# The reciprocal root of the variance moves from ScalarE to GpSimd

## The chip, the cores and the metric

The kernel runs on one core of a Trainium2 chip. The metric is the device time of one execution in microseconds (us). The kernel before takes 2158.09 us (median of three runs, 2158.0 to 2159.71). Five engines work side by side, each through its own queue of instructions in order: PE (TensorE, matrix multiplications; its weight loads are shown as PEld), DVE (VectorE), ACT (ScalarE), POOL (GpSimd) and SP (SyncE, which issues the DMAs here). They meet only at semaphores.

## The reference, cut to what matters

Four "triangle" layers follow each other on an image x of 256 x 256 tokens with 64 channels. Each adds its result to x, after a group normalisation over pairs of channels (`_gn`). Three of the four (layers 0, 1 and 3) begin with a layer norm over the 64 channels of each token:

```python
xn = (x - mean(x)) * rsqrt(var(x) + 1e-5) * g + b         # per token, over 64 channels
left  = xn @ Wl.T * m * sigmoid(xn @ Wlg.T)               # m: a mask per token, layers 0 and 1
right = xn @ Wr.T * m * sigmoid(xn @ Wrg.T)
out_gate = sigmoid(xn @ Wog.T)
out = einsum('bikd,bjkd->bijd', left, right)              # the triangle product
x = x + (layernorm(out) * out_gate) @ Wout.T
```

The change touches only how `rsqrt(var + eps)` of that first layer norm is computed. Layer 2 has no such norm on its input.

## The kernel before, in words

x lies as 128 partitions (two halves of the image, 64 channels each) by 32768 tokens. Each layer has three stages: the projection (`project`, L435; layer 2 has its own), the triangle product, and the output. In the trace the projections of layers 0, 1 and 3 run roughly from 58 to 370 us, 660 to 980 us and 1523 to 1844 us.

`project` takes the tokens in 64 chunks of 512 columns. Sixteen chunks make one turn of a loop (BODY), and eight chunks make one batch (BATCH), so a projection has 8 batches and the program has 24. Each engine has a function `step(i, q, more)` that it runs for every chunk q, with leads: the constants on L444 say how many chunks ahead of the chunk in hand a part is done. The parts are:

- PE, in this order in each step (L602): `spread` of chunk q+4 (NORM), `center` of chunk q+14, `heads` of chunk q for its two rows of 256 tokens, `out_gate` of chunk q, and `variance` of chunk q+13. `variance` (L561) adds the squares over channels into one PSUM tile, VAR; after eight chunks it holds a 16 x 512 tile, one batch. `spread` (L572) multiplies the reciprocal roots out over the channels into PSUM tile R; it first waits for `r_split` of its batch.
- ACT (L661): `square` (two activations, L635 and L637, for chunk q+14), two sigmoids of the gates (L654), `root` where a batch has just been completed (q is 2 or 10), and then the sigmoid of the output gate (L671). `out_gate` of the next chunk on PE waits until that last sigmoid has read the PSUM tile GATE.
- `root` (L639): loads the table set that has logarithm and exponential, waits for the batch's last `variance`, and computes exp(-0.5 * ln(var + eps)) in two activations, L644 and L647. The sigmoid after it needs its own table set again, and a load is placed in front of it.
- DVE (L745): `norm` of chunk q+4 (three or so tensor operations, which wait for `spread`), `split_r` where q+5 is a multiple of 8 (q is 3 or 11), and `left_and_right` of chunk q (L742, two instructions, which wait for the sigmoids and free the PSUM pair that `heads` of the next chunk writes). `split_r` (L691) waits for `r_done` and splits r into three bfloat16 terms by five instructions (L699 to L706).
- POOL, in layers 0 and 1 alone (L761): multiplies the product by the mask, after `left_and_right` of the same chunk. In layer 3 POOL has nothing to do in the projection.

Before the loop, PE and ACT run 14 chunks of `center`, `square` and `variance` alone, and the first `root` and `split_r` of a projection lie there.

Of the kernel before, what the change touches and what calls it, by code (L numbers as in the profile page):

```python
# [28 lines left out]
ALU = mybir.AluOpType  # L29
ACT = mybir.ActivationFunctionType  # L30
AXIS = mybir.AxisListType

P = 128
# [3 lines left out]
CH = 512  # L37
NCH = HALF * S // CH
ROWS = CH // S
SEG = 16  # L40
SCH = SEG // ROWS
BODY = 2 * SCH
BATCH = 8
# [4 lines left out]
LN_SET = "natural_log_exp_and_others"  # L48
# [19 lines left out]
def build(nc, a, out):  # L68

    with ExitStack() as ctx:  # L70
        def sb(name, shape, dt=F32):
            return ctx.enter_context(nc.sbuf_tensor(name, shape, dt))

        def counter(name, base=FIRST):
            return Counter(ctx.enter_context(nc.semaphore(name)), base)

        k = {
            "basis": sb("basis", [P, P]), "var_w": sb("var_w", [P, 4 * BATCH - 2]), "ident": sb("ident", [P, P]),
            "pool_w": sb("pool_w", [P, P]), "last_row": sb("last_row", [2, P]), "unit": sb("unit", [P, 3]),
            "gn": sb("gn", [P, 12]), "gn_stats": sb("gn_stats", [P, NCH, 6]), "gn_sums": sb("gn_sums", [P, 2, NCH]),  # L80
            "vec": sb("vec", [P, NVEC]), "center": sb("center", [P, P]), "shift": sb("shift", [P, 1]),
            "w_out": sb("w_out", [P, P]),
            "out_bias": sb("out_bias", [P, 1]), "one": sb("one", [1, P]),

            "mask": sb("mask", [P, 2, 2, P]),
        }
        ps = [ctx.enter_context(nc.psum_tensor(f"ps{n}", [P, 2, 512], F32)) for n in range(4)]

        c = {n: counter(n) for n in (
            "fold_vec", "fold_mm", "fold_act", "stat_done", "z_done", "sq_done", "var_done", "log_done", "r_done", "r_part", "r_split", "spread_done",  # L90
            "xn_done", "hi_done", "lo_done", "proj_done", "gate_mm_done", "sig_done", "gate_done", "masked", "lr_done", "pair_read",
            "tr_done", "tr_copied", "tri_done", "packed", "o_copied", "o_stored", "o_moved",
            "ln_stat", "ln_root", "ln_scale", "centered", "scaled", "wt_done", "wt_copied", "gated",
            "out_mm_done", "u_cleared", "out_gated", "x_new", "counted", "aggregated")}

        for n, ring in (("const_in", 1), ("x_in", 8), ("lr_out", 2), ("first_out", 2), ("gate_out", 4), ("lr_in", 2),
                        ("xc_in", 4), ("gc_in", 4), ("x_out", 4)):
            for i in range(ring):
                c[f"{n}{i}"] = counter(f"{n}{i}", 16)
        start_counters(nc, c, k, a)  # L100
        first_statistics(nc, a, c, k)
        x = a["x"]
        for n, kind in enumerate(("masked", "masked_bf16", "plain", "normed")):
            x_new = out if n == 3 else a[f"x_dram{n % 2}"]
            layer(nc, n, kind, a, x, x_new, c, k, ps)
            x = x_new
# [95 lines left out]
class Fold:  # L202
# [53 lines left out]
    def step(self, dve, ins):  # L256

        self.steps += 1
        ins.then_inc(self.done.sem, 1)
        dve.wait_ge(self.done.sem, self.done(self.steps))  # L260
# [155 lines left out]
SEG_PARTS = 8  # L416
# [18 lines left out]
def project(nc, n, kind, low, HG, x, a, left_right, blocks, c, k, ps):  # L435
# [5 lines left out]

    LOAD, CENTER, VARIANCE, SPLIT, NORM = 16, 14, 13, 5, 4  # L444
    masked, gate = kind != "normed", a["gate"]
    with ExitStack() as ctx:
        def sb(name, shape, dt=F32):
# [7 lines left out]
        sig, gates = sb("sig", [P, 4, CH]), sb("gates", [P, 4, CH])  # L455
        paired = low == BF16
# [24 lines left out]
        def staged(b, q, row):  # L481

            at = q % SCH * ROWS + row
            return stage[b].rearrange("p g b l n (h i) -> p (g b) (l n h) i", h=HG)[:, :, :, at]
# [145 lines left out]
        def _(act):  # L630
# [8 lines left out]
            def root(i, b):  # L639

                batch = i * (BODY // BATCH) + b
                act.preload_act_table_set(LN_SET)
                act.wait_ge(c["var_done"].sem, c["var_done"](batch * BATCH + BATCH))
                act.activation(log_var[:], VAR, ACT.Ln, bias=k["unit"][0:2 * BATCH, 2:3]).then_inc(c["log_done"].sem, 1)  # L644
                act.wait_ge(c["log_done"].sem, c["log_done"](batch + 1))
                act.wait_ge(c["r_split"].sem, c["r_split"](batch))
                act.activation(r[:], log_var[:], ACT.Exp, scale=-0.5).then_inc(c["r_done"].sem, 1)  # L647

            def gate_pair(i, q, row):
                m = i * BODY + q  # L650
# [107 lines left out]
                norm(0, q)  # L758
            bodies_of(dve, step)

        if masked:  # L761
            @block.gpsimd
            def _(pool):
                def mask_pair(i, q, row):
                    m = i * BODY + q
                    b = q // SCH
                    if q % SCH == 0 and row == 0:

                        pool.wait_ge(c[f"lr_out{b}"].sem, c[f"lr_out{b}"](i * 16 * SEG_PARTS))
                        pool.wait_ge(c[f"first_out{b}"].sem, c[f"first_out{b}"](i * 64))  # L770
                    pool.wait_ge(c["pair_read"].sem, c["pair_read"](m * 2 + row + 1))
                    product = sig[:, (2 * q + row) % 4, :].rearrange("p (a e) -> p a e", a=4)

                    by_g = k["mask"][:].rearrange("p g b i -> p (g b) i")
                    mk = by_g[:, :, bass.ds(m * ROWS + row, 1)].to_broadcast([P, 4, P])
                    pool.tensor_tensor(staged(b, q, row), product, mk,
                                       ALU.mult).then_inc(c["lr_done"].sem, 1)

                def mask_rows(i, q):
                    m = i * BODY + q  # L780
                    b = q // SCH
                    if q % SCH == 0:
                        pool.wait_ge(c[f"lr_out{b}"].sem, c[f"lr_out{b}"](i * 16 * SEG_PARTS))
                        pool.wait_ge(c[f"first_out{b}"].sem, c[f"first_out{b}"](i * 64))
                    pool.wait_ge(c["pair_read"].sem, c["pair_read"](m * 2 + 2))
                    slot, at = 2 * q % 4, q % SCH * ROWS
                    product = sig[:, slot:slot + 2, :].rearrange("p r (c e) -> p c e r", c=4)
                    by_g = k["mask"][:].rearrange("p g b i -> p (g b) i")
                    mk = by_g[:, :, bass.ds(m * ROWS, ROWS)].unsqueeze(2).to_broadcast([P, 4, P, ROWS])
                    rows = stage[b].rearrange("p g b l n (h i) -> p (g b) (l n h) i", h=HG)[:, :, :, at:at + ROWS]  # L790
                    pool.tensor_tensor(rows, product, mk, ALU.mult).then_inc(c["lr_done"].sem, 2)

                with pool.Fori(0, bodies) as i:
                    for q in range(BODY):
                        if paired:
                            mask_rows(i, q)
                        else:
                            for row in range(ROWS):
                                mask_pair(i, q, row)

    fold.finish()
    for s in range(4):
# [621 lines left out]
def constants():  # L1424

    basis = np.zeros((C, C), np.float32)
    for m in range(C - 1):
        basis[:m + 1, m] = 1 / np.sqrt((m + 1) * (m + 2))
        basis[m + 1, m] = -(m + 1) / np.sqrt((m + 1) * (m + 2))
    live = (np.arange(P) % C != C - 1)  # L1430
    group = np.arange(P) % C // 2
    var_w = np.zeros((P, 4 * BATCH - 2), np.float32)
    spread = np.zeros((P, BATCH, P), np.float32)
    for g in range(2):
        half = slice(g * C, g * C + C)
        var_w[half, 2 * BATCH - 2 + g] = live[half] / C
        for q in range(BATCH):
            for part in range(3):
                spread[R_PART * part + 2 * q + g, q, half] = live[half]
    spread[R_ONE] = ~live  # L1440
    unit = np.zeros((P, 3), np.float32)
    unit[:, 0] = ~live
    unit[:, 1] = np.where(live, EPS, 1)
    unit[:, 2] = EPS
    h_center = {}
    for n, H in ((2, 16), (3, C)):
        h_center[f"h_center{n}"] = np.zeros((P, P), np.float32)
        h_center[f"h_center{n}"][:2 * H, :2 * H] = np.kron(np.eye(2), np.eye(H) - 1 / H)
    last_row = np.zeros((2, P), np.float32)
    last_row[0, C - 1] = last_row[1, P - 1] = 1  # L1450
    return {
        **h_center, "basis": np.kron(np.eye(2), basis), "var_w": var_w, "spread": spread.reshape(P, BATCH * P), "ident": np.eye(P),
        "pool_w": (group[:, None] == group[None, :]) / 4, "last_row": last_row, "unit": unit, "one": np.ones((1, P)),
    }
# [90 lines left out]
```

## Time and profile before

| | |
|---|---|
| median of 3 runs | 2158.09 us |
| the profiled execution: its own time | 2161.47 us |
| its span, first to last instruction | 2159.6 us |
| mean granted TensorE clock over the span | 0.96 of full speed |
| busy share of the span: PE, DVE, ACT, POOL | 83%, 71%, 61%, 37% |

A row of the timeline gives the start in us, the duration in us, the engine, the line of the kernel, the operation, what it writes and reads, and how many instructions the row merges. What stands in brackets is the idle time of the engine just before it, and what ended it. A row of the groups ends with busy us in total and the mean in ns, and then the idle time before them.

### The profile page before, as it was taken

Reading aid. Unit: us, or ns where it says so; the run is one execution under the profiler, and the core shown is the slowest. Engines: PE = TensorE matmul, PEld = TensorE weight load, DVE = VectorE, ACT = ScalarE, POOL = GpSimd, SP = SyncE. Lnnn points to the kernel's source line nnn. Section 1 sums busy time; section 2 is a strip of 40 time slices with the busy share of each in tenths; the row PEclk is TensorE's granted clock in tenths of the full one; section 3 lists DMA queues with packets and bytes.
Section 4 is the critical chain, followed back from the end, with each engine's and each line's share of the span. In section 5 each row is a group of like instructions: output and inputs, shape, how many; then the busy total and the mean of one; then the engine's idle time right before and its main releaser. Section 6 shows DMA issues by size and latency. Waiting matters only on the chain. (4 is left out here: it accounts for less than half of the span.)

```text
span 2159.6 us, 40771 instructions
## 1 busy us (share of the span) xinstructions
PE 1792.7 (83%) x10305; PEld 966.5 (45%) x10389; DVE 1522.9 (71%) x3171; ACT 1310.5 (61%) x2413; POOL 808.0 (37%) x740
## 2 busy tenths in 40 slices
PE   0899996897998999965699799877799997699665
PEld 0234343785552343433355476633233333588332
DVE  7588887225754999996876487588488889344775
ACT  0577775466994777755599576433377776344322
POOL 0044445006980444445799100288000000000799
PEclk9999999898999999998899899999899999899999
DMA  7367777775994446446499686299447776754799
GB/s 316 118 190 224 241 217 219 292 311 175 362 369 137 137 156 194 156 147 234 152 366 360 228 293 225 95 396 398 151 149 222 236 231 207 266 232 161 246 354 333
DMA packets 336162, 512.88 MB, mean 237 GB/s; under 512 B 23979, under 2 KB 189486, under 8 KB 329654
## 3 DMA queue, kind: packets, MB, share of 16 engines
q1 hardware_dynamic: 336054, 511.65, 69.3%
q8 instruction: 42, 0.69, 0.1%
q14 instruction: 66, 0.54, 0.1%
HBM read 293.46 MB, written 205.52 MB: 231 GB/s over the span
## 5 line engine op out<-in xcount | busy, mean ns | idle before, releaser
L1289 POOL TENSOR_TENSOR shared<-O,out_rs 128x128 f32<-128x128 f32 (+1 forms) x128 | 94.9, 743 | 687.3 <-DVE out_rs L1196 686.1
L591 PE MATMUL ps<-w_heads,hi 64*128 64x256 f16 x3072 | 292.1, 273 | 36.3 <-DVE sig L742 25.2
L654 ACT ACTIVATE sig<-ps,largest 128x512 f32<-128x512 f32 x384 | 246.8, 692 | 51.3 <-PE ps L591 49.8
L1087 ACT ACTIVATE O<-ps 128x512 f32 (+1 forms) x144 | 151.9, 1055 | 183.5 <-PE ps L1008 183.5
L635 ACT ACTIVATE zs<-ps,shift 128x512 f32<-128x512 f32 x192 | 131.9, 687 | 213.0 <-PE ps L559 213.0
L1333 PE MATMUL ps<-ident,shared 128*128 128x128 f32 (+1 forms) x1024 | 163.3, 284 | 107.9 <-POOL shared L1289 107.8
L1333 PEld LDWEIGHTS ps<-ident,shared 128*128 128x128 f32 (+1 forms) x1024 | 114.3, 133 | 278.3 <-POOL shared L1289 194.2
L591 PEld LDWEIGHTS ps<-w_heads,hi 64*128 64x128 f16 x3072 | 154.1, 95 | 181.3 <-issue 65.8
L559 PE MATMUL ps<-xs,center 128*128 128x512 f32 x384 | 204.7, 615 | 13.6 <-issue 10.4
L591 PE MATMUL ps<-w_heads,lo 64*128 64x256 f16 x1536 | 213.0, 272 | 0.0
L742 DVE SCALAR_TENSOR_TENSOR sig<-ps,largest,sig 128x512 f32<-128x512 f32 x256 | 179.9, 743 | 46.1 <-ACT sig L654 44.5
L570 PE MATMUL ps<-sq,var_w 128*16 128x512 f32 x384 | 200.2, 603 | 4.3 <-ACT log_var L644 4.3
L1188 DVE BATCH_NORM_STATS2 out_bn<-O 128x6 f32 (+2 forms) x1024 | 193.9, 257 | 12.5 <-PEq L941 12.3
L1008 PE MATMUL ps<-shared,packed 128*128 128x256 f32 (+1 forms) x768 | 154.9, 356 | 47.2 <-DVE packed L1032 46.8
L1032 DVE COPY packed<-shared 128x512 f32<-128x512 f32 (+1 forms) x208 | 96.6, 491 | 126.4 <-PE ps L1008 43.3
L728 DVE TENSOR_TENSOR lo<-xn,hi 128x512 f16<-128x512 f32 x192 | 180.4, 940 | 6.6
L1275 POOL TENSOR_TENSOR shared<-O,out_bn 128x512 f32<-128x512 f32 x128 | 134.9, 1054 | 132.3 <-DVE out_bn L1188 132.3
L1300 POOL TENSOR_TENSOR shared<-shared 128x512 f32<-128x512 f32 x128 | 165.0, 1291 | 28.9 <-DMA x_dram<-shared 15.1
L1375 ACT ACTIVATE shared<-ps 32x512 f32<-32x512 f32 (+1 forms) x128 | 75.5, 590 | 154.1 <-PE ps L1333 154.1
L1008 PEld LDWEIGHTS ps<-shared,packed 128*128 128x128 f32 (+1 forms) x768 | 121.2, 164 | 81.3 <-DVE packed L1032 31.5
L1205 DVE TENSOR_TENSOR shared<-ps,shared 128x512 f32<-128x512 f32 x128 | 88.5, 692 | 96.5 <-ACT ps L1371 93.6
L1008 PE MATMUL ps<-shared,right_t 128*128 128x256 f32 x640 | 153.1, 385 | 3.7 <-DVE right_t L1039 3.6
(156 smaller groups left out, 3635.0 us busy)
## 6 DMA issues: line engine op xcount, KB each, us to landing
shared<-left_right SPq DMA_DIRECT2D x34, 2048.0 KB, 10.1
shared<-gate SPq DMA_DIRECT2D x256, 256.0 KB, 4.5
gate<-gates SPq DMA_DIRECT2D x96, 512.0 KB, 2.9
x_dram<-shared SPq DMA_DIRECT2D x192, 256.0 KB, 4.4
shared<-x_dram SPq DMA_DIRECT2D x192, 256.0 KB, 4.7
xs<-x_dram SPq DMA_DIRECT2D x64, 512.0 KB, 4.1
left_right<-stage SPq DMA_DIRECT2D x64, 448.0 KB, 5.8
left_right<-shared SPq DMA_DIRECT2D x64, 448.0 KB, 5.7
```

The lines of the kernel that those rows point to most:

```text
L559: pe.matmul(bank, k["center"][:], xs[:, q % 8, :], start=True, stop=True).then_inc(c["z_done"].sem, 1)
L570: pe.matmul(VAR, w, sq[:, q % 2, :], start=(at == 0), stop=(at == BATCH - 1)).then_inc(c["var_done"].sem, 1)
L591: last = pe.matmul(PAIR[row][:, g, kb * S:kb * S + S], tokens[half, q % 8, at:at + P], k["w_heads"][half, part, :], start=(step == 0), sto ...
L654: act.activation(sig[:, slot, :].rearrange("p (c e) -> p c e", c=4), pair(row, 0), ACT.Sigmoid, scale=k["largest"][:, 0:1]).then_inc(c["si ...
L728: dve.tensor_tensor(lo[:, q % 8, :], xn[:, q % 2, :], hi[:, q % 8, :], ALU.subtract).then_inc(c["lo_done"].sem, 1)
L742: dve.scalar_tensor_tensor(dst, pair(row, 1), k["largest"][:, 1:2], factor, ALU.mult, ALU.mult).then_inc(pair_read.sem, 1)
L1008: last = pe.matmul(ps[h % 4 // 2][:, h % 2, jb * S:jb * S + S], stationary, moving, start=(kb == 0), stop=(kb == 1))
L1087: act.activation(o_of(ch), ps[h % 4 // 2][:, h % 2, :].rearrange("p (b g i) -> p b g i", b=2, g=2), ACT.Copy).then_inc(c["o_copied"].sem, 1)
L1188: last = dve.bn_stats(bn[:, b, jb, at:at + 2, :].rearrange("p g s -> p (g s)"), tokens.rearrange("p g h -> p h g"))
L1275: pool.tensor_tensor(centered[:, q % RING], rows[:, :, bass.ds(m * 2 * ROWS, 2 * ROWS), :], per_token(bn[:, :, :, :, 1:2], q), ALU.subtrac ...
L1300: pool.tensor_tensor(xo[:, q % RING, :], og[:, q % RING], xs[:, q % RING, :], ALU.add).then_inc(c["x_new"].sem, 1)
L1333: last = pe.transpose(TURNED[q % 4][:, at:at + P], scaled[:, q % RING, jb, 2 * row:2 * row + 2, :].rearrange("p g h -> p (g h)"), k["ident ...
```

## The change

ScalarE's `root` keeps one activation: it adds eps to the variance (Identity with a bias) and writes it to the same tile `log_var` in SBUF. The table load and the logarithm and exponential are gone. GpSimd gets `inverse_root`: one TENSOR_TENSOR on 16 x 512 elements whose operation is power, with the constant -0.5 (a new column of `unit`, broadcast) as second operand. It stands in POOL's step where q+5 is a multiple of 8, ahead of the mask of that chunk, and once ahead of the loop. POOL now has a queue in layer 3 too, and its loop has the same form as that of the other engines. The functions for the mask are unchanged apart from indentation.

```diff
-            "pool_w": sb("pool_w", [P, P]), "last_row": sb("last_row", [2, P]), "unit": sb("unit", [P, 3]),
+            "pool_w": sb("pool_w", [P, P]), "last_row": sb("last_row", [2, P]), "unit": sb("unit", [P, 4]),
...
-    LOAD, CENTER, VARIANCE, SPLIT, NORM = 16, 14, 13, 5, 4
+    LOAD, CENTER, VARIANCE, ROOT, SPLIT, NORM = 16, 14, 13, 5, 5, 4
...
             def root(i, b):
                 batch = i * (BODY // BATCH) + b
-                act.preload_act_table_set(LN_SET)
                 act.wait_ge(c["var_done"].sem, c["var_done"](batch * BATCH + BATCH))
-                act.activation(log_var[:], VAR, ACT.Ln, bias=k["unit"][0:2 * BATCH, 2:3]).then_inc(c["log_done"].sem, 1)
-                act.wait_ge(c["log_done"].sem, c["log_done"](batch + 1))
-                act.wait_ge(c["r_split"].sem, c["r_split"](batch))
-                act.activation(r[:], log_var[:], ACT.Exp, scale=-0.5).then_inc(c["r_done"].sem, 1)
+                act.wait_ge(c["r_done"].sem, c["r_done"](batch))
+                act.activation(log_var[:], VAR[0:2 * BATCH, :], ACT.Identity, bias=k["unit"][0:2 * BATCH, 2:3]).then_inc(c["log_done"].sem, 1)
...
-        if masked:
-            @block.gpsimd
-            def _(pool):
+        @block.gpsimd
+        def _(pool):
...
+            def inverse_root(i, b):
+                batch = i * (BODY // BATCH) + b
+                pool.wait_ge(c["log_done"].sem, c["log_done"](batch + 1))
+                pool.wait_ge(c["r_split"].sem, c["r_split"](batch))
+                pool.tensor_tensor(r[:], log_var[:], k["unit"][0:2 * BATCH, 3:4].to_broadcast([2 * BATCH, CH]), ALU.pow).then_inc(c["r_done"].sem, 1)
+
+            def step(i, q, more):
+                if more(ROOT) and (q + ROOT) % BATCH == 0:
+                    inverse_root(i, (q + ROOT) // BATCH)
+                if paired:
+                    mask_rows(i, q)
+                elif masked:
+                    for row in range(ROWS):
+                        mask_pair(i, q, row)
+
+            inverse_root(0, 0)
+            bodies_of(pool, step)
...
-    unit = np.zeros((P, 3), np.float32)
+    unit = np.zeros((P, 4), np.float32)
+    unit[:, 3] = -0.5
```

## Rows read from the trace of the kernel before

**Rows 1.** Stretches: length; busy (count) of PE, PEld, DVE, ACT, POOL; clock; DMA; GB/s.
```profile
182.00:218.00 36.00, 33.92 (x253) 14.43 (x256) 29.59 (x46) 27.89 (x45) 16.70 (x17) 1.00 0.77 235
823.00:859.00 36.00, 34.00 (x254) 14.36 (x257) 34.04 (x46) 27.81 (x45) 16.34 (x8) 1.00 0.55 172
```

**Rows 2.** Timeline of PE in layer 0, around a root.
```profile
169.21 0.39 PE L578 MATMUL ps<-r_terms,spread 128*128 128x512 bf16 x1
173.52 0.39 PE L578 MATMUL ps<-r_terms,spread 128*128 128x512 bf16 x1
...
181.18 1.03 PE L570 MATMUL ps<-sq,var_w 128*16 128x512 f32 x2
182.14 0.39 PE L578 MATMUL ps<-r_terms,spread 128*128 128x512 bf16 x1
...
186.25 0.39 PE L598 MATMUL ps<-hi,w_gate 128*128 128x512 f16 x1 [1.45 <-ACT gates L671]
```

**Rows 3.** Groups by line and form: the table loads and the logarithm.
```profile
L642 ACT ACT_TABLE_LOAD x24 | 30.8, 1283 | 0.4
L671 ACT ACT_TABLE_LOAD x21 | 26.9, 1283 | 0.4
L644 ACT ACTIVATE log_var<-ps,unit 16x512 f32<-16x512 f32 x24 | 16.3, 679 | 0.3
```

**Rows 4.** Timeline of DVE and POOL in layer 0, around the same root.
```profile
184.59 0.41 DVE L699 CAST r_terms<-r 16x512 bf16<-16x512 f32 x1
...
186.49 0.68 DVE L706 TENSOR_TENSOR r_terms<-r_rest,r_mid 16x512 bf16<-16x512 f32 x1
...
181.92 2.09 POOL L776 TENSOR_TENSOR stage<-sig,mask 128x512 f32<-128x512 f32 x2 [2.23 <-DVE sig L742]
```

**Rows 5.** Timeline of PE, DVE and POOL in layer 1, around a root.
```profile
822.88 0.39 PE L578 MATMUL ps<-r_terms,spread 128*128 128x512 bf16 x1
...
825.82 0.41 DVE L699 CAST r_terms<-r 16x512 bf16<-16x512 f32 x1
...
823.31 2.04 POOL L791 TENSOR_TENSOR shared<-sig,mask 128x1024 bf16<-128x1024 f32 x1 [2.27 <-DVE sig L742]
```

**Rows 6.** Timeline of PE and DVE in layer 3, around a root.
```profile
1688.54 0.39 PE L578 MATMUL ps<-r_terms,spread 128*128 128x512 bf16 x1
...
1691.01 0.41 DVE L699 CAST r_terms<-r 16x512 bf16<-16x512 f32 x1
```

**Rows 7.** Timeline of ACT and PEld at the first root of layer 0.
```profile
83.48 1.28 ACT L642 ACT_TABLE_LOAD   x1
...
85.49 0.63 ACT L647 ACTIVATE r<-log_var 16x512 f32<-16x512 f32 x1
...
88.84 0.10 PEld L578 LDWEIGHTS ps<-r_terms,spread 128*128 128x128 bf16 x1 [1.13 <-DVE r_terms L706]
```

**Rows 8.** Groups by line and form: elementwise work of POOL and DVE, and a reciprocal.
```profile
L1289 POOL TENSOR_TENSOR shared<-shared,out_rs 128x512 f32<-128x512 f32 x128 | 133.5, 1044 | 20.9 <-DVE out_rs L1196 20.9
L885 DVE TENSOR_TENSOR biased<-ps,mask 128x512 f32<-128x512 f32 x64 | 44.3, 692 | 11.7 <-PE ps L863 4.3
L889 DVE TENSOR_TENSOR product<-biased 128x256 f32<-128x256 f32 x64 | 27.2, 425 | 2.2
L1289 POOL TENSOR_TENSOR shared<-O,out_rs 128x128 f32<-128x128 f32 x64 | 25.6, 402 | 194.1 <-DVE out_rs L1196 192.9 <-PE ps L1333 1.0
L1196 DVE RECIPROCAL out_rs<-out_std 128x32 f32<-128x32 f32 x32 | 10.9, 340 | 0.0
L1196 DVE RECIPROCAL out_rs<-out_std 128x64 f32<-128x64 f32 x16 | 8.8, 552 | 2.3 <-ACT out_std L1383 2.2
```

**Rows 9.** Stretches at a pause of PE before layer 3's output stage; columns as in rows 1.
```profile
2005.00:2012.00 7.00, 0.12 (x2) 0.11 (x2) 5.50 (x28) 2.64 (x3) 1.20 (x2) 0.84 0.64 199
2012.00:2015.00 3.00, 3.00 (x13) 2.42 (x14) 3.00 (x16) 1.40 (x3) 2.85 (x3) 0.50 0.64 238
2015.00:2022.00 7.00, 6.69 (x23) 2.96 (x21) 5.21 (x18) 2.61 (x5) 5.23 (x5) 0.89 0.37 110
```

More of the change, by code:

```diff
@@ L759, in _ @@
             bodies_of(dve, step)
-        if masked:
-            @block.gpsimd
-            def _(pool):
[L764 to L799, printed above, removed]
@@ new lines, in _, with mask_pair, mask_rows @@
+        @block.gpsimd
+        def _(pool):
+            def mask_pair(i, q, row):
+                m = i * BODY + q
+                b = q // SCH
+                if q % SCH == 0 and row == 0:
+                    pool.wait_ge(c[f"lr_out{b}"].sem, c[f"lr_out{b}"](i * 16 * SEG_PARTS))
+                    pool.wait_ge(c[f"first_out{b}"].sem, c[f"first_out{b}"](i * 64))
+                pool.wait_ge(c["pair_read"].sem, c["pair_read"](m * 2 + row + 1))
+                product = sig[:, (2 * q + row) % 4, :].rearrange("p (a e) -> p a e", a=4)
+                by_g = k["mask"][:].rearrange("p g b i -> p (g b) i")
+                mk = by_g[:, :, bass.ds(m * ROWS + row, 1)].to_broadcast([P, 4, P])
+                pool.tensor_tensor(staged(b, q, row), product, mk,
+                                   ALU.mult).then_inc(c["lr_done"].sem, 1)
+            def mask_rows(i, q):
+                m = i * BODY + q
+                b = q // SCH
+                if q % SCH == 0:
+                    pool.wait_ge(c[f"lr_out{b}"].sem, c[f"lr_out{b}"](i * 16 * SEG_PARTS))
+                    pool.wait_ge(c[f"first_out{b}"].sem, c[f"first_out{b}"](i * 64))
+                pool.wait_ge(c["pair_read"].sem, c["pair_read"](m * 2 + 2))
+                slot, at = 2 * q % 4, q % SCH * ROWS
+                product = sig[:, slot:slot + 2, :].rearrange("p r (c e) -> p c e r", c=4)
+                by_g = k["mask"][:].rearrange("p g b i -> p (g b) i")
+                mk = by_g[:, :, bass.ds(m * ROWS, ROWS)].unsqueeze(2).to_broadcast([P, 4, P, ROWS])
+                rows = stage[b].rearrange("p g b l n (h i) -> p (g b) (l n h) i", h=HG)[:, :, :, at:at + ROWS]
+                pool.tensor_tensor(rows, product, mk, ALU.mult).then_inc(c["lr_done"].sem, 2)
+            def inverse_root(i, b):
[13 more added lines that the diff above has]
+            bodies_of(pool, step)
```

## The prediction

> **What bounds the kernel now.** I read the page's busy shares first, then the stretches of a projection, then the timelines of each engine around one root. The stretches of 36 us, one batch of eight chunks each, have PE busy for 33.9 and 34.0 us at full clock, ACT for only 27.9 and 27.8 us, DVE for 29.6 and 34.0 us [rows 1]. So PE bounds the projection. In the timeline of PE two `spread` matmuls that follow each other lie 173.52 - 169.21 = 4.31 us apart, which is one chunk [rows 2]. The reader is to see that this step is whole but for one place per batch: at 186.25 us PE has stood idle for 1.45 us, released by ACT's sigmoid L671 [rows 2]. That sigmoid was late because ACT first loaded a table, took logarithm and exponential and loaded the other table. The same stall, 1.45 to 1.52 us long, stands at the roots that I looked at in layers 1 and 3. There are 7 such roots in each of three projections (the first root lies ahead of the loop), so the whole prize on PE is about 21 x 1.5 = 32 us. What ACT loses in busy time is more, but it is not what ends anything.
>
> **What goes from ACT.** 45 table loads of 1.283 us and 24 exponentials of 0.63 us [rows 3, 7], together 73 us of ACT time. The Identity that replaces the logarithm has its form and reads the same PSUM tile, so I cost it at the logarithm's 0.679 us [rows 3]. The load for a projection's first sigmoid stays. Around a root, the last `variance` starts at 181.18 us and is done at 182.2 [rows 2]; Identity then runs to 182.95, the sigmoid L671 to about 183.7, and PE wants GATE free at 180.43 + 4.31 = 184.7. The stall on ACT goes whole; ACT has about 1 us of cover left. What is late next is r itself.
>
> **What comes on POOL, and the new chain.** The chain is now: last `variance`, Identity on ACT, power on POOL (call its duration D), `split_r` on DVE, `spread` on PE. The split's five instructions take 186.49 + 0.68 - 184.59 = 2.58 us [rows 4]. `spread` of the next batch is the first thing in PE's next step, so everything on PE queues behind it. And POOL takes the power only after the mask of the chunk before, because it stands behind it in its queue. I take 0.1 us for each of the two semaphore steps. The stall S of PE at one root, against its undisturbed step:
>
> - Layer 0: the mask ends at 181.92 + 2.09 = 184.01 [rows 4]; the split ends at 184.01 + D + 0.1 + 2.58 = 186.69 + D; PE wants it at 182.14 + 4.31 = 186.45 [rows 2]. S = D + 0.33.
> - Layer 1: mask ends 823.31 + 2.04 = 825.35, PE wants r at 822.88 + 4.31 = 827.19 [rows 5]. S = D + 0.94.
> - Layer 3: no mask, so POOL starts when Identity ends. `variance` precedes `spread` by 0.96 us and ends about when `spread` starts [rows 2], so at about 1688.6; Identity ends at 1689.4; PE wants r at 1688.54 + 4.31 = 1692.85 [rows 6]. S = D - 0.67.
>
> There is a floor, since DVE doesn't reach the split before it has done `norm` of the chunk in front: it got there at 184.59, 825.82 and 1691.01 [rows 4 to 6], which gives S of at least 0.8, 1.3 and 0.85 us whatever D is. So even a free power leaves half of the old stall.
>
> Against the 1.5 us that go, the 7 roots of each projection cost 7 x (D - 1.17), 7 x (D - 0.56) and 7 x (D - 2.17), together 21 D - 27.3 us. The first root of a projection: Identity can start at about 83.5 where the load stood, and end at 84.2, while the exponential ended at 86.12 [rows 7]; PE's `spread` waited for the split there, so r comes D - 1.9 later, three times: 3 D - 5.7. The sum is **24 D - 33.0 us**, and zero at D = 1.4.
>
> What else is queued: behind the power on POOL is the mask of the same chunk, which needs DVE's `left_and_right`, itself behind the split, so it isn't later on the power's account. Behind the split on DVE is that `left_and_right`, which frees PE's PSUM pair; PE needs it only 1.2 us after `spread`, and its first half takes 0.7. SP's stores have whole chunks of lead. These edits cost nothing beyond S.
>
> **What D is.** No power stands in the trace. The lower end is a plain product on POOL with 512 elements per partition, 1.04 us [rows 8]; that the tile has 16 partitions and not 128 should not shorten it. At that D the sum is 24 x 1.04 - 33 = -8, and with layer 3's floors about -4 us. The upper end: a power is a logarithm, a product and an exponential; if each of some 20 elementary steps cost POOL one pass of 1.04 us, D is 21 us and the sum +470. Between them I go by the one row of an operation that isn't a single step: DVE's reciprocal costs (552 - 340) / 32 = 6.6 ns per element, DVE's product (692 - 425) / 256 = 1.04 ns, which is 6.4 times less. POOL's product costs (1044 - 402) / 384 = 1.67 ns per element [rows 8], so 6.4 times that for 512 elements is 5.5 us, and with 0.2 us of fixed cost D = 5.7 us. That makes 24 x 5.7 - 33 = +104 us.
>
> The Trainium skill, "GPSIMD Engine Reference", section 3.1, has no price for a power. It says that a two-input body is bound by the read port at about 2.6 cycles per element, and that longer bodies go at about three operations a cycle. An estimate from that page is 1.1 us if the power were as short as a product, which is the second case below, and 5.7 us if it has some 40 operations.
>
> **The clock.** Stalls of 6 us are longer than any that the projection has now. Where PE stood for nearly 7 us, its granted clock was 0.84 in that stretch, 0.50 (the 1.2 GHz level) in the 3 us after it, and 0.89 in the next 7 [rows 9]. That is 3 + 7 x 0.11 / 0.5 = 4.5 us at half speed, or 2.3 us of lost work, and PE is the bound there. For 21 stalls: +48 us. If the clock doesn't drop it is 0.
>
> **The sum.** 104 + 48 = +152 us on the profiled execution's 2161.5 (span 2159.6), which is 3.4 above the median of the runs: 2158 + 152 = **2310 us**.
>
> **The rivals.**
>
> 1. *The power is several times dearer than a product* (the forecast, D from 1.8 to 16 us). For it: everything that isn't a single step costs a multiple in the rows. 64%.
> 2. *The power costs what a product costs*, D about 1.05. The stall on r replaces the stall on the sigmoid almost one for one: 2158 - 4 = 2154 us, within 0.2%. For it: POOL's products cost the same per element whatever they read. Against it: they are single steps. 13%.
> 3. *The stall falls to DVE's floor*, because the power is ready when `norm` ends. That is the faster side, and one mechanism: with D under 1.1 us and POOL free to take it beside the mask's tail, each root keeps only 0.8, 1.3 or 0.85 us of its 1.5, and the first roots give up to 1.5 each: -(7 x (0.7 + 0.2 + 0.65) + 3 x 1.5) = -15 us, 2143. It decides below D = 1.2; above 1.4 it is lost. 12%.
> 4. *A power far dearer than my rows*, D over 16 us: over 24 x 16 - 33 + 48 = +400, so 2560 and more. For it: a chain of dependent steps in software. 10%.
> 5. *ACT's time is the bound after all*, and its 73 us come back: 2085. Against it: ACT is idle for 8 of 36 us [rows 1]. 1%. The Trainium skill, "ScalarE: Activation LUTs", section "Rules for kernel authors", tells one to group functions by table set and puts a switch at about 2.7 us with its drain. By that, 45 switches would be some 120 us. The trace has 1.283 us for a load and 0.4 us of idle time before all 24 of L642 [rows 3], so no drain is seen.
>
> That the change doesn't take the loads away is excluded: Identity, Square and Sigmoid already alternate with no load between them, apart from the first sigmoid and those behind a root.
>
> **How the numbers follow.** A measurement of this kernel can tell about 0.2%, 4.3 us, from no change. Slower holds case 1, case 4 and a part of case 2: 0.75. Same is most of case 2: 0.11. Faster is cases 3 and 5 and what my floors may miss: 0.14. The range reaches down to case 2 and up to D = 15.5, that is 24 x 15.5 - 33 + 48 = +387: **2150 to 2550**. Case 1's own range is 2168 (D = 1.8, clock kept) to 2550.
>
> **What would show it.** Right: ACT has no load but the first of each projection, and its sigmoid L671 follows Identity at once; PE's long wait at a root stands at `spread` (L578), released by DVE's split, which waited for POOL's power; 24 rows of it with a mean near 5.7 us; a period of about 42 us between roots instead of 36; a dip of the clock after each. Wrong: a power of about 1 us, with stalls near 1 us at `spread`; or a PE stall that stays at the sigmoid; or stalls shorter in layer 1 than in layer 3, which would mean that the mask in front of the power doesn't count.

## The result

The changed kernel takes 4139.9 us (median of 4 runs, 4138.5 to 4144.4) against 2158.5 us for the kernel before (the three runs above and one more): a ratio of 1.918 (95% interval 1.915 to 1.921), 1981 us slower. The prediction was 2310 us with a range of 2150 to 2550. The direction was right and the size was off by 1830 us.

The profiled execution has a span of 4136.6 us. Its page, first the busy shares, then the three costliest groups of instructions, of which the first is new:

```profile
PE 1846.6 (45%) x10389; PEld 980.5 (24%) x10389; DVE 1528.9 (37%) x3171; ACT 1239.6 (30%) x2344; POOL 2777.2 (67%) x764
...
L793 POOL TENSOR_TENSOR r<-log_var,unit 16x512 f32<-16x512 f32 x24 | 1970.5, 82104 | 406.0 <-ACT log_var L644 406.0
L578 PE MATMUL ps<-r_terms,spread 128*128 128x512 bf16 x192 | 80.5, 419 | 1983.0 <-DVE r_terms L703 1979.5
L696 DVE CAST r_terms<-r 16x512 bf16<-16x512 f32 x24 | 10.0, 415 | 1955.3 <-POOL r L793 1955.3
```

One row is the result: 24 powers of 82.1 us each, 1970.5 us in all. The two rows under it are the chain that waits for it. DVE's split stood idle for 1955 us until POOL's power ended, and PE's `spread` for 1979.5 us until the split ended. PE's work grew by only 54 us.

The groups by form of ACT's loads and of the Identity, which answer [rows 3]:

```profile
L644 ACT ACTIVATE log_var<-ps,unit 16x512 f32<-16x512 f32 x24 | 16.2, 676 | 16.8 <-PE ps L570 16.8
L651 ACT ACT_TABLE_LOAD x3 | 3.8, 1283 | 0.1
```

The 24 loads ahead of the root and the 21 behind it are gone; the load of the first sigmoid of each projection stayed. Identity costs 676 ns where the logarithm cost 679. ACT is busy for 71 us less. The change does what it says.

The timelines around a root in layer 0 (start, us, engine, line), which answer [rows 2, 4]: ACT, then POOL, DVE and PE.

```profile
190.50 0.68 ACT L644 ACTIVATE log_var<-ps,unit 16x512 f32<-16x512 f32 x1 [0.71 <-PE ps L570]
191.09 0.66 ACT L668 ACTIVATE gates<-ps,largest 128x512 f32<-128x512 f32 x1
...
190.17 2.09 POOL L772 TENSOR_TENSOR stage<-sig,mask 128x512 f32<-128x512 f32 x2 [1.67 <-DVE sig L739]
192.19 81.91 POOL L793 TENSOR_TENSOR r<-log_var,unit 16x512 f32<-16x512 f32 x1
...
274.24 0.42 DVE L696 CAST r_terms<-r 16x512 bf16<-16x512 f32 x1 [80.47 <-POOL r L793]
...
276.96 0.61 PE L578 MATMUL ps<-r_terms,spread 128*128 128x512 bf16 x1 [82.18 <-DVE r_terms L703]
...
1785.01 0.60 PE L578 MATMUL ps<-r_terms,spread 128*128 128x512 bf16 x1 [83.27 <-DVE r_terms L703]
3309.71 0.61 PE L578 MATMUL ps<-r_terms,spread 128*128 128x512 bf16 x1 [81.41 <-DVE r_terms L703]
```

The order is the predicted one. ACT's sigmoid follows Identity at once, the power starts only when the mask (which began at 190.17) is done, 1 us after Identity, and PE waits 82.18 us at `spread`. The formula of the prediction for this layer, S = D + 0.33, gives 82.2 with the 81.91 us of this power. The last two rows are roots of layers 1 and 3: PE waits 83.27 and 81.41 us there, where the formulas D + 0.94 and D - 0.67 give 83.3 and 81.2 with the powers of these two roots, 82.36 and 81.91 us.

The stretches around the same root, which answer [rows 1, 9] (length, busy of PE, PEld, DVE, ACT, POOL with counts, granted clock, DMA share, GB/s):

```profile
192.00:274.00 82.00, 2.78 (x25) 1.02 (x21) 1.73 (x2) 2.76 (x5) 82.00 (x2) 0.54 0.04 13
274.00:280.00 6.00, 3.04 (x11) 1.32 (x13) 5.47 (x10) 0.61 (x2) 2.17 (x3) 0.50 0.00 0
280.00:284.00 4.00, 4.00 (x28) 1.50 (x22) 2.52 (x5) 2.69 (x5) 1.66 (x2) 0.96 0.00 0
```

All engines but POOL stand still through the first stretch. PE restarts at 276.96 at a granted clock of 0.50 (the 1.2 GHz level) and is back at full clock soon after 280: some 3.4 us at half speed, 1.7 us lost.

### The profile page after: what moved, and what is told of

It is laid out like the page before. It is cut to its first block and busy times, and to the rows that moved or that the text cites. A ratio compares the mean times of both kernels' runs of the same rounds, so it can differ in the third digit from the quotient of the medians.

```text
span 4136.6 us, 40755 instructions
## 1 busy us (share of the span) xinstructions
PE 1846.6 (45%) x10389; PEld 980.5 (24%) x10389; DVE 1528.9 (37%) x3171; ACT 1239.6 (30%) x2344; POOL 2777.2 (67%) x764
## 5 line engine op out<-in xcount | busy, mean ns | idle before, releaser
L793 POOL TENSOR_TENSOR r<-log_var,unit 16x512 f32<-16x512 f32 x24 | 1970.5, 82104 | 406.0 <-ACT log_var L644 406.0
L578 PE MATMUL ps<-r_terms,spread 128*128 128x512 bf16 x192 | 80.5, 419 | 1983.0 <-DVE r_terms L703 1979.5
L696 DVE CAST r_terms<-r 16x512 bf16<-16x512 f32 x24 | 10.0, 415 | 1955.3 <-POOL r L793 1955.3
L578 PEld LDWEIGHTS ps<-r_terms,spread 128*128 128x128 bf16 x192 | 18.7, 97 | 2132.3 <-issue 1121.8
L591 PE MATMUL ps<-w_heads,hi 64*128 64x256 f16 x3072 | 306.8, 282 | 28.7 <-DVE sig L739 19.9
L559 PE MATMUL ps<-xs,center 128*128 128x512 f32 x384 | 223.8, 668 | 1.0 <-DVE shift L346 1.0
L725 DVE TENSOR_TENSOR lo<-xn,hi 128x512 f16<-128x512 f32 x192 | 173.8, 905 | 6.6
```

What stands on the lines that cost most here:

```text
L559: pe.matmul(bank, k["center"][:], xs[:, q % 8, :], start=True, stop=True).then_inc(c["z_done"].sem, 1)
L591: last = pe.matmul(PAIR[row][:, g, kb * S:kb * S + S], tokens[half, q % 8, at:at + P], k["w_heads"][half, part, :], start=(step == 0), sto ...
L725: dve.tensor_tensor(lo[:, q % 8, :], xn[:, q % 2, :], hi[:, q % 8, :], ALU.subtract).then_inc(c["lo_done"].sem, 1)
L793: pool.tensor_tensor(r[:], log_var[:], k["unit"][0:2 * BATCH, 3:4].to_broadcast([2 * BATCH, CH]), ALU.pow).then_inc(c["r_done"].sem, 1)
```

## The experiments

Where an experiment's time is set against 2158.5 us below, it is its own ratio times that. The kernel before had a median of 2160.0 us in the first group of runs, 2160.1 in the second and 2159.7 in the last.

**What a power costs.** The kernel before, with a block of nine POOL operations ahead of its layers:

```diff
+            for n, (parts, cols, at, op) in enumerate((
+                    (16, 512, 0, ALU.pow), (16, 256, 0, ALU.pow), (16, 64, 0, ALU.pow), (4, 512, 0, ALU.pow),
+                    (32, 512, 0, ALU.pow), (128, 512, 0, ALU.pow), (128, 64, 0, ALU.pow),
+                    (16, 512, 1, ALU.pow), (16, 512, 0, ALU.mult))):
+                pool.wait_ge(ready, 3 + n)
+                pool.tensor_tensor(powed[0:parts, 0:cols], probe[0:parts, 0:cols],
+                                   half[0:parts, at:at + 1].to_broadcast([parts, cols]), op).then_inc(ready, 1)
```

> The kernel before, with a block ahead of its layers in which POOL takes nine operations one after the other, each waiting for the one before: powers of 16x512, 16x256, 16x64, 4x512, 32x512, 128x512, 128x64 elements with exponent -0.5, one of 16x512 with exponent 2, and a product of 16x512. All inputs are 0.7. Theory A (each of GpSimd's cores works on its 16 partitions as one vector, 160 ns per column): 82, 41, 10.4, 82, 82, 82, 10.4 us; exponent 2 again 82; product about 1.05. Rival B (elements of a core go one after the other, 10 ns each): 4x512 takes 20.5 us, the others as in A. Rival C (elements of all partitions one after the other): 32x512 takes 164 us and 128x512 takes 656 us. Rival D (cost hangs on the exponent or the value): exponent 2 far below 82, or -0.5 of a constant far from 82.

Its groups by form (busy us, mean ns, idle before):

```profile
L177 POOL TENSOR_TENSOR powed<-probe,half 16x512 f32<-16x512 f32 x3 | 164.9, 54951 | 53.0 <-DVEq L157 52.8
L177 POOL TENSOR_TENSOR powed<-probe,half 128x512 f32<-128x512 f32 x1 | 81.9, 81931 | 0.1
L177 POOL TENSOR_TENSOR powed<-probe,half 32x512 f32<-32x512 f32 x1 | 81.9, 81906 | 0.1
L177 POOL TENSOR_TENSOR powed<-probe,half 4x512 f32<-4x512 f32 x1 | 81.9, 81905 | 0.1
L177 POOL TENSOR_TENSOR powed<-probe,half 16x256 f32<-16x256 f32 x1 | 41.1, 41111 | 0.1
L177 POOL TENSOR_TENSOR powed<-probe,half 128x64 f32<-128x64 f32 x1 | 10.5, 10520 | 0.1
L177 POOL TENSOR_TENSOR powed<-probe,half 16x64 f32<-16x64 f32 x1 | 10.5, 10506 | 0.1
```

From 64 to 256 columns is 192 columns and 30.6 us: 160 ns per column, with 0.3 us of fixed cost. Partitions are free from 4 to 128. The three 16x512 operations sum to 164.9 us; the shortest of this line is the product with 1.03 us, so two powers of 81.9 us are left, and the exponent 2 costs what -0.5 costs. All inputs of this block are 0.7; the changed kernel's own variances gave the same 82 us. Theory A's numbers hold; rivals B, C and D fall. The whole execution took 2634.6 us in a single run.

**Only the duration, or the place too.** The changed kernel with a product for the power:

```diff
-                pool.tensor_tensor(r[:], log_var[:], ....to_broadcast([2 * BATCH, CH]), ALU.pow)
+                pool.tensor_tensor(r[:], log_var[:], ....to_broadcast([2 * BATCH, CH]), ALU.mult)
```

> The changed kernel with a product in place of the power, in the same place and form; the reciprocal root is thereby left out, so values differ and no time but the operation's own should. Theory A (the power's own duration is the whole loss, and the sum 24 D - 33 with DVE's floors holds): D falls from 82.1 to about 1.05 us, the stalls at spread (L578) to 1.4, 2.0 and 0.85 us in layers 0, 1 and 3, and the time is about 2154 us (2148 to 2162). Rival B (the place of the root in POOL's queue, between masks and behind two more semaphores, costs something of its own): above 2175 us even with a product. Rival C (ACT's freed 73 us matter once the power is out of the way): below 2130 us.

Measured: 2170.9 us, ratio 1.0053 (1.0036 to 1.0070), so 11 us slower than before where -4 was expected. With D at 1.03 to 1.54 us (1.2 in the mean), 1970 of the 1981 us are gone: the place costs little. But even an operation as cheap as a product does not gain, and 15 us needed another cause. From the sixth to the last `norm` of each projection, layer 0 is 2 us longer than in the kernel before, layer 1 is 11 us longer and layer 3 is 2 us shorter. The rows of four roots, two of layer 0 and one each of layers 1 and 3, show what differs; after each block's DVE rows stand POOL's and, in layer 1, PE's:

```profile
183.20 1.54 DVE L725 TENSOR_TENSOR lo<-xn,hi 128x512 f16<-128x512 f32 x1
184.66 0.41 DVE L696 CAST r_terms<-r 16x512 bf16<-16x512 f32 x1
183.16 1.03 POOL L793 TENSOR_TENSOR r<-log_var,unit 16x512 f32<-16x512 f32 x1
...
219.30 0.69 DVE L725 TENSOR_TENSOR lo<-xn,hi 128x512 f16<-128x512 f32 x1
221.03 0.41 DVE L696 CAST r_terms<-r 16x512 bf16<-16x512 f32 x1 [1.03 <-POOL r L793]
219.34 1.54 POOL L793 TENSOR_TENSOR r<-log_var,unit 16x512 f32<-16x512 f32 x1
...
832.96 0.41 DVE L696 CAST r_terms<-r 16x512 bf16<-16x512 f32 x1 [1.03 <-POOL r L793]
831.33 1.48 POOL L793 TENSOR_TENSOR r<-log_var,unit 16x512 f32<-16x512 f32 x1
835.99 1.91 PE L559 MATMUL ps<-xs,center 128*128 128x512 f32 x2 [2.70 <-DVE r_terms L703]
...
1666.06 0.84 DVE L723 CAST hi<-xn 128x512 f16<-128x512 f32 x1
1665.58 1.03 POOL L793 TENSOR_TENSOR r<-log_var,unit 16x512 f32<-16x512 f32 x1 [35.08 <-ACT log_var L644]
```

POOL's product and the last operations of DVE's `norm` lengthen each other. In four of the seven roots of layer 0 the product started 0.01 to 0.05 us before L725 (L728 in the kernel before), and L725 took 1.54 to 1.57 us instead of 0.69. In the other three, and in all seven of layer 1, L725 had started first and POOL's product took 1.48 to 1.54 us instead of 1.03; DVE then waited about 1 us for it. In layer 3 the cast L723 took 0.60 to 0.86 us instead of 0.43. By the prediction's chain with a 1.03 us operation, the split should start 3.00, 3.60 and 2.47 us after the last `spread` in layers 0, 1 and 3; in most roots it started after 3.29 or 3.47, 4.05, and 2.81 to 2.98 us. That is 0.3 to 0.5 us per root, some 9 us in all.

The second part is the clock: after three of layer 1's waits (3.75, 2.70 and 2.71 us) PE restarted at the 1.2 GHz level, and its two matmuls L559 took 1.91 us where they take 1.02 at full clock; by the granted clock in half-microsecond stretches each of the three lost 1.3 to 1.5 us, some 4 us in all. It stayed full after the other three of layer 1 (2.54 to 2.62 us) and after those of layers 0 and 3 (1.4 to 2.0 us); the last root of each projection is left out of this count. Together that is an estimate of 13 of the 15 us, read from rows; no run takes either part away by itself.

**Is the floor the order of spread and split.** The product run with NORM at 3:

```diff
-    LOAD, CENTER, VARIANCE, ROOT, SPLIT, NORM = 16, 14, 13, 5, 5, 4
+    LOAD, CENTER, VARIANCE, ROOT, SPLIT, NORM = 16, 14, 13, 5, 5, 3
```

> As the product run, but NORM is 3 instead of 4: norm and spread of a chunk come one chunk later, while the root and the split stay where they are; the reciprocal root is left out. Theory A (the floor that I set on the stall comes from spread being queued right behind the split): the stall at spread goes, and what is left is DVE's left_and_right behind the split, 0.3, 0.8 and 0.65 us by layer; about 2134 us (2125 to 2145). Rival B (PE has other waits at a root, not seen behind the old one): no better than the product run, 2150 or more.

Measured: 2166.3 us, ratio 1.0029 (1.0014 to 1.0043). It gained 5 us on the product run and missed 2134 widely. Rival B holds: the wait moved from `spread` to `heads` in PE's next work.

```profile
185.97 0.28 PE L591 MATMUL ps<-w_heads,hi 64*128 64x256 f16 x2 [1.27 <-DVE sig L739]
...
180.97 1.54 DVE L725 TENSOR_TENSOR lo<-xn,hi 128x512 f16<-128x512 f32 x1
```

In layer 0 PE waits 1.27 us here for `left_and_right` behind the split (1.45 at every second root) where I had set 0.3; in most roots of layers 1 and 3 it waits 2.03 and 1.1 to 1.3 us where I had set 0.8 and 0.65. The lengthened L725 is there again, 0.85 us of the 1.27.

**The assumed duration.** The changed kernel with a power on the first columns and a product on the rest, for a planned D of 5.8 us (28 columns) and 11.4 us (64 columns); the reciprocal root is left out for the other columns:

```diff
-                pool.tensor_tensor(r[:], log_var[:], ....to_broadcast([2 * BATCH, CH]), ALU.pow)
+                pool.tensor_tensor(r[:, 0:28], log_var[:, 0:28], ....to_broadcast([2 * BATCH, 28]), ALU.pow)
+                pool.tensor_tensor(r[:, 28:CH], log_var[:, 28:CH], ....to_broadcast([2 * BATCH, CH - 28]), ALU.mult)
```

> The changed kernel, but the power is taken of the first 28 columns only and the other 484 get a product; the root is thereby left out for them. At the measured 160 ns per column D is 4.5 + 0.3 + 1.0 = 5.8 us, the value that the prediction had assumed. Theory A (only D was wrong; 24 D - 33 and about 2.3 us of lost clock at each of 21 stalls hold): 2158 + 106 + 48 = 2312 us (2295 to 2330). Rival B (the clock doesn't drop for 6 us stalls): 2264 us. Rival C (something besides D and the clock grows with the power's share, for instance contention of POOL with DVE): above 2340 us.

> As before with 64 columns of power and 448 of product: D is 10.5 + 0.9 = 11.4 us. Theory A: 2158 + 24 x 11.4 - 33 + 48 = 2447 us, that is 24 us for each us of D above the run with 28 columns, and no further loss of clock. Rival B (the loss of clock grows with the length of the stall): more than 15 us above that line.

Measured: 2314.7 us, ratio 1.0727 (1.0704 to 1.0749), and 2449.9 us, ratio 1.1354 (1.1331 to 1.1378), where 2312 and 2447 were expected. Power and product together took 5.95 and 11.6 us in the mean. These two runs and the changed kernel lie on one line: +157 us at 5.95, +292 at 11.6, +1981 at 82.1 us, which is 23.8 and 24.0 us per us of D. Rivals B and C of the one and B of the other fall. What is left above 24 D - 33 is 47, 46 and 44 us, and it does not grow with the stall. The stretches of the 28-column run around a root show where most of it lies, columns as above:

```profile
209.00:211.00 2.00, 0.00 (x0) 0.00 (x0) 1.92 (x4) 0.00 (x0) 0.00 (x0) 0.68 1.12 348
211.00:216.00 5.00, 4.34 (x26) 2.39 (x27) 3.82 (x7) 1.96 (x3) 2.08 (x2) 0.50 0.32 115
216.00:217.00 1.00, 1.00 (x7) 0.23 (x3) 0.56 (x1) 0.64 (x1) 0.27 (x1) 0.73 0.00 0
```

PE stands idle when the granted clock falls, restarts at 211.66 and has full clock again from about 216.5: 4.9 us at half speed, 2.4 us lost. Read in half-microsecond stretches, the stalls at the roots lost 1.2 to 2.7 us each in this run, 1.3 to 2.9 in the 64-column run and 1.4 to 3.1 in the changed kernel, with means of 1.9, 2.0 and 2.2 us. Over 21 stalls that is 40 to 47 us. That is read from the rows; no run holds the clock at full speed through such a stall.

**The power on all 128 partitions.** SP moves the variances to 128 partitions x 64 columns, POOL takes the power there, SP moves the roots back:

```diff
+                sp.wait_ge(c["log_done"].sem, c["log_done"](batch + 1))
+                sp.dma_start(wide_in[:], log_var[:].rearrange("p (a e) -> p a e", a=8)).then_inc(c["wide_moved"].sem, 16)
...
+                sp.wait_ge(c["r_done"].sem, c["r_done"](batch + 1))
+                sp.dma_start(r[:].rearrange("p (a e) -> p a e", a=8), wide_out[:]).then_inc(c["r_moved"].sem, 16)
...
+                pool.wait_ge(c["wide_moved"].sem, c["wide_moved"](batch * 16 + 16))
+                pool.tensor_tensor(wide_out[:], wide_in[:], k["unit"][:, 3:4].to_broadcast([P, CH // 8]), ALU.pow)
```

> The change made with all of GpSimd's cores: SP moves the 16 x 512 variances to 128 partitions x 64 columns by a DMA, POOL takes the power there (10.5 us for 64 columns), and a second DMA moves the roots back; the result is whole. Theory A (cost is 160 ns per column, and a small DMA takes about 3 us from issue to landing as gate<-gates does): D in the chain is 10.5 + 2 x 3 = 16.5 us and the time 2158 + 24 x 16.5 - 33 + 48 = 2569 us (2500 to 2640), so 1570 of the 1981 us come back. Rival B (the wide form costs more than it gives, because SP's queue holds the moves up): above 2700 us.

Measured: 2554.0 us, ratio 1.1826 (1.1801 to 1.1851), where 2569 was expected. The power took 10.5 us, the moves 3.2 and 2.0 us in the median from issue to landing. The 3.2 is a mixture: the way out took 2.1 us in layer 1 and 5.4 to 5.6 us in layers 0 and 3 (medians). Of the 1981 us, 1587 came back through the other layout, the moves included. Theory A holds.

**The wide power with a lead.** The same with NORM 1 and SPLIT 2, the way back two chunks later:

```diff
-    LOAD, CENTER, VARIANCE, ROOT, SPLIT, NORM = 16, 14, 13, 5, 5, 4
+    LOAD, CENTER, VARIANCE, ROOT, SPLIT, NORM = 16, 14, 13, 5, 2, 1
```

> The wide power with a lead: NORM is 1 instead of 4 and SPLIT 2 instead of 5, so that spread wants the roots three chunks (12.9 us) later; SP moves them back two chunks later than it moves the variances out. The result is whole. Theory A (the chain's length against its lead is all that counts): most of the 16 us chain is covered, DVE waits about 2 us at the split, and about 24 x 12.9 = 310 us come back: 2245 us (2215 to 2290), still slower than the kernel before, because POOL's mask of the next chunk stands behind a 10.5 us power in layers 0 and 1. Rival B (POOL's 10.5 us block the masks, the sigmoids' slots and so PE as much as the chain did): above 2350 us.

Measured: 2311.8 us, ratio 1.0698 (1.0678 to 1.0717). 243 us came back, not 310. In layer 0, from 100 to 340 us, the waits (us in all, times, longest) show that the power now holds up other work, and PE's rows show what is left in layers 0 and 3:

```profile
ACT sig L668 <- POOL stage L789: 19.6, 5, 8.0
...
223.19 0.40 PE L608 MATMUL ps<-w_heads,hi 64*128 64x256 f16 x2 [5.84 <-DVE sig L756]
1799.56 0.61 PE L595 MATMUL ps<-r_terms,spread 128*128 128x512 bf16 x1 [5.03 <-DVE r_terms L720]
```

ACT waited up to 8.0 us for a mask that stood behind the power in POOL's queue, as rival B says. In most roots of layer 0 PE still waits 5.5 to 6.1 us at `heads` and 0.9 to 1.6 at `spread`, in layer 1 some 3.0 to 3.3 us at `heads` and 1.1 to 2.8 at `spread`. Layer 3, which has no mask, waits 4.9 to 5.1 us at `spread`: its move out took 5.5 us in the median where 3 were assumed, and its power up to 11.0 us. The first root of each projection, ahead of the loop, is followed by a wait of about 10 us (10.46, 10.38 and 9.80). So theory A's 2 us per root were too few, and rival B's wait for the mask is there in the layers that have one; the time lies between both theories' numbers.

**What the old stall was made of.** The kernel before with ACT's root behind the sigmoid of the output gate, alone and with NORM at 3:

```diff
-                root_step(i, q, more)
                 act.wait_ge(c["gate_mm_done"].sem, c["gate_mm_done"](m + 1))
...
                 act.activation(gates[:, q % 4, :], GATE, ACT.Sigmoid, scale=k["largest"][:, 2:3]).then_inc(c["gate_done"].sem, 1)
+                root_step(i, q, more)
```

> The kernel before with one edit: ACT takes the root (loads, logarithm, exponential) behind the sigmoid of the output gate instead of ahead of it. Theory A (ACT's block of 3.9 us stalls PE in the projection wherever it stands, since ACT has only about 1 us of slack per chunk and feeds PE through single buffers): the wait at L598 goes, one of about 1.2 us comes at spread or center; about 2154 us (2148 to 2160). Rival B (the stall was only the order of sigmoid and root): all 1.5 us of 21 roots go, about 2127 us.

> The kernel before with ACT's root behind the sigmoid of the output gate and NORM 3 instead of 4, so that neither the gate's sigmoid nor spread waits for the root. Theory A (ACT's block of two table loads, logarithm and exponential, 3.9 us against about 1 us of slack per chunk, stalls the loop through its other buffers, whichever wait is taken away): about 2153 us, 1.2 us of stall left per root. Rival B (the stall was in those two waits alone): about 2128 us.

Measured: 2159.1 us, ratio 0.9998 (0.9988 to 1.0008), and 2156.6 us, ratio 0.9986 (0.9976 to 0.9996). The first is no change that can be told; PE's wait at the root has moved from L598 to `spread`, 1.3 to 1.5 us at nearly all roots (here 1.33). The second is 3 us faster than the kernel before and the fastest of this study, though within the 0.2% named in the prediction. Theory A holds for both: PE's wait at L598 is gone, and in the second kernel another stands at `heads`, released by DVE, behind ACT's block. The first row is from the first kernel, the others from the second:

```profile
186.21 1.02 PE L559 MATMUL ps<-xs,center 128*128 128x512 f32 x2 [1.33 <-DVE r_terms L706]
...
180.41 1.28 ACT L642 ACT_TABLE_LOAD   x1
184.21 1.28 ACT L654 ACT_TABLE_LOAD   x1
185.50 1.27 ACT L654 ACTIVATE sig<-ps,largest 128x512 f32<-128x512 f32 x2
...
187.03 0.28 PE L591 MATMUL ps<-w_heads,hi 64*128 64x256 f16 x2 [1.05 <-DVE sig L742]
```

The sigmoids of the next chunk come late by the second load, DVE's product with them, and PE's pair is freed 1.05 us late (1.4 to 1.5 in layer 3).

## Why the prediction was wrong

Step by step, as the prediction put them:

- **"What D is": this step failed.** I bounded the power by a product (1.04 us) and by 20 passes of a product (21 us) and took 5.7 us from the ratio of DVE's reciprocal to DVE's product. It measured 82.1 us, 4 times my upper end and 14 times my value. The ratio came from another engine, and the upper end from a count of elementary steps that no row gave, and the chain multiplies an error in D by 24. Per column the power costs 160 ns where POOL's product costs 1.67 ns [rows 8]: a factor of 96, not 6.4.
- **The chain and the sum 24 D - 33: right for D of 5.8 us and more.** With D = 82.1 it gives +1937 us, and with the clock's 48 us +1985. Measured: +1981. It was tested at 5.95, 11.6 and, by way of two DMAs, at some 16 us.
- **The floor at small D: too low.** For a product it gave -4 us against +11 measured. I had left out that POOL's operation falls on DVE's last operations of `norm` and that the two lengthen each other, by 0.3 to 0.5 us per root on this chain, and that three of layer 1's waits (2.70 to 3.75 us) cost clock. Case 2 of the rivals, "one for one", was nearer to the truth than case 3, which was held by nothing that ran: even with the operation nearly free, no run with it was faster than before.
- **What goes from ACT: right.** 45 loads and the exponentials went and 71 us of ACT's time with them, and PE's wait at the gate's sigmoid went. Rival 5 is excluded by the product run: 75 us of ACT's time were free there, and the time did not fall.
- **The clock, +48 us: right in size.** 1.9 to 2.2 us per stall were read in the mean where I had 2.3.
- **The chances.** Case 4, a power over 16 us, held 10% and is what happened, and the range left it out. Why a power takes 160 ns per column, in dependent steps or otherwise, no run shows. A range whose upper end rests on a guess for an operation that the trace doesn't show should have been open to 100 us per operation, or the forecast given as a line in D alone.

## What to carry to other kernels

An operation that no row of the trace shows is to be measured by itself before it is placed on a chain, most of all when it isn't one arithmetic step; its price by another engine's ratio is no bound. The power's time on GpSimd went by its columns and not by its partitions, so a 16-partition tile of such an operation is better laid over all 128 first: 10.5 us and two moves took the place of 82. And a stall that one engine's block causes in a tight loop need not go when the block is moved: here 1.0 to 1.5 us of the old 1.5 came back at the next wait, once at `spread` and once at `heads`.

## What the runs showed of the hardware

- A power by TENSOR_TENSOR on GpSimd took 0.3 us + 160 ns per column in float32, the same for 4, 16, 32 and 128 partitions and, at an input of 0.7, for exponents -0.5 and 2. A product of 16x512 took 1.03 us.
- A DVE operation with two inputs from SBUF (L725) took 1.54 us where a POOL TENSOR_TENSOR of only 16 partitions had started 0.04 us before it, and 0.69 us alone. Where L725 had started 0.04 us earlier, it took 0.69 us and POOL's 1.03 us product took 1.54. Beside the 81.91 us power that began at 192.19, the L725 of 192.23 took 1.53 us, so it did not wait for the power's end. DVE's cast L723 took 0.84 us beside POOL's product and 0.43 alone.
- A DMA of 32 KB within SBUF, between 16 x 512 and 128 x 64, took 2.0 us from issue to landing on the way back, and on the way out 2.1 us in layer 1 and 5.4 to 5.6 us in layers 0 and 3 (medians by layer).
